# Windowed and latent attention: transposes, rotations and a reciprocal square root take other places in the instruction order

## The reference, cut to what matters

```python
def attn_layer(x, Wqkv, qs, ksc, Wo):
    q, k, v = split(x @ Wqkv)                 # 16 heads of 64
    q = l2norm(q) * qs ; k = l2norm(k) * ksc
    q = q * cos * scale + rotate_half(q) * sin * scale
    k = k * cos / scale + rotate_half(k) * sin / scale
    return local_attention(q, k, v) @ Wo      # softmax over 2 windows of 32
for i in range(6):
    x = attn_layer(shift_tokens(x), ...) + x
    x = ffn_layer(shift_tokens(x), ...) + x   # layer norm, a * gelu(gate)
```

```python
q_c, kv = heads(x) @ W_DQ.T @ W_UQ.T, heads(x) @ W_DKV.T @ W_UKV.T
q = concat(rms_norm(q_c, wq), rms_norm(q_c, wq) @ W_QR.T)
k = concat(rms_norm(k_c, wk), heads(x) @ W_KR.T)
out = softmax(q @ k.T * scale + causal) @ v_c @ W_O.T
```

## Time and profile before

| | |
|---|---|
| median of 3 runs | 6266.62 us (6263.59 to 6266.95) |
| profiled execution | 6259.03 us, span 6257.3 us |
| busy over the span | PE 87%, DVE 68%, ACT 63%, POOL 43% |
| windowed transformer, L1766 first and last start | 642.8 to 5275.1 us |
| latent attention, L1377 first and last start | 5418.5 to 5649.3 us |

### The profile page before, as it was taken

How to read it: one execution, slowest core, us unless ns; L and a number is a source line. 1 busy time by engine, 2 the same in 40 slices (tenths; PEclk the granted TensorE clock), 3 DMA queues, 4 the chain that set the end, 5 groups by cost and what they waited for, 6 DMA issues and landing times. The chain is left out here.

```text
span 6257.3 us, 121573 instructions
## 1 busy us (share of the span) xinstructions
PE 5454.5 (87%) x41154; PEld 3791.3 (61%) x41154; DVE 4256.5 (68%) x16112; ACT 3942.9 (63%) x11510; POOL 2699.1 (43%) x2578
## 2 busy tenths in 40 slices
PE   7885799999999999997489999999999999687989
PEld 5673466666666666665256666666666666454678
DVE  4453777777777877875477777787787777444522
ACT  2211677777777778774177777777777877221333
POOL 0000555555555555552165555555555555220000
PEclk9996899999999999998599999999999999787999
DMA  0000000000000000000000000000000000000000
GB/s 11 22 1 2 21 1 15 6 11 9 7 10 6 11 9 11 8 1 4 21 1 10 9 3 11 9 11 9 1 15 6 11 8 1 5 2 4 2 28 8
DMA packets 30964, 53.45 MB, mean 9 GB/s; under 512 B 7688, under 2 KB 17168, under 8 KB 29712
## 3 DMA queue, kind: packets, MB, share of 16 engines
q1 hardware_dynamic: 30352, 45.66, 2.3%
HBM read 44.60 MB, written 1.05 MB: 7 GB/s over the span
## 5 line engine op out<-in xcount | busy, mean ns | idle before, releaser
L1785 PE MATMUL bank<-wA,next_rowT 128*128 128x512 f32 x2304 | 1185.6, 624 | 272.7 <-DVE turnB L2126 164.0
L1982 ACT ACTIVATE pairs<-pairs,negmax 128x128 f32<-128x128 f32 (+1 forms) x3072 | 1240.4, 420 | 19.0 <-DVE negmax L2087 15.6
L1959 POOL TENSOR_TENSOR turnA<-raw,ropes 128x512 f32<-128x512 f32 x768 | 968.7, 1272 | 243.8 <-ACT raw L2006 214.8
L2087 DVE CUSTOM_DVE_ANT_0 pairs<-bank,bands,big 128x128 f32<-128x128 f32 (+1 forms) x3072 | 941.4, 362 | 86.4 <-PE bank L1717 82.9
L1966 POOL TENSOR_TENSOR qk<-turnA,turnB 128x512 f32<-128x512 f32 x768 | 976.9, 1272 | 0.0
L1785 PEld LDWEIGHTS bank<-wA,next_rowT 128*128 128x128 f32 x2304 | 377.1, 190 | 719.2 <-DVE turnB L2126 378.9
L1943 POOL COPY spread<-recip 128x256 f32<-128x256 f32 x768 | 305.7, 398 | 965.0 <-DVE recip L2096 958.0
L1972 POOL TENSOR_TENSOR qk<-qk,big 128x1024 f32<-128x1024 f32 x192 | 365.6, 1904 | 739.0 <-DVE recip L2201 739.0
L1989 ACT ACTIVATE pairsT<-bank 128x512 f32<-128x512 f32 x768 | 469.2, 611 | 337.3 <-PE bank L1730 337.1
L1982 ACT ACTIVATION_READ_ACCUMULATOR pairs<-pairs,negmax 128x1 f32 x3072 | 631.2, 205 | 0.0
L285 POOL TENSOR_TENSOR rstd<-vareps,neg_half 128x2 f32<-128x2 f32 x56 | 39.0, 696 | 1287.1 <-DVE vareps L256 888.0
(11 more groups left out here) (306 smaller groups left out, 11229.7 us busy)
## 6 DMA issues: line engine op xcount, KB each, us to landing
wA<-in_wt_wqkv SPq DMA_DIRECT2D x72, 256.0 KB, 2.8
wB<-in_wt_wo SPq DMA_DIRECT2D x12, 512.0 KB, 3.5
wC<-in_wt_w SPq DMA_DIRECT2D x12, 341.0 KB, 2.9
wD<-in_wt_w SPq DMA_DIRECT2D x12, 192.0 KB, 2.4
big<-in_e_up SPq DMA_DIRECT2D x1, 2048.0 KB
big<-in_e_down SPq DMA_DIRECT2D x1, 2048.0 KB
scl<-in_wt_scales SPq DMA_DIRECT2D x12, 128.0 KB, 3.1
X<-in_x SPq DMA_DIRECT2D x8, 128.0 KB, 2.5
```

The lines of the kernel that those rows point to most:

```text
L1785: pe.matmul(side_bank(i)[:, :], c.next_rowT[:, t * P:(t + 1) * P], wqkv[:, k * 512:(k + 1) * 512], start=True, stop=True).then_inc(s.chunk ...
L1959: g.tensor_tensor(c.turnA[:, m % 2, :].rearrange("p (h d) -> p h d", h=8), c.raw[:, m % 4, :].rearrange("p (h d) -> p h d", h=8), cos, ALU ...
L1982: last = a.activation(tile, tile, ACT.Exp, scale=-1.0, bias=c.negmax[:, 2 * p + side, t:t + 1], accum_out=c.pair_sums[:, p % 4, t, side:si ...
L2087: last = v.tensor_tensor_reduce(c.pairs[:, 2 * (p % 4) + side, AT[t]:AT[t] + SPAN[t]], c.bank[side][:, AT[t]:AT[t] + SPAN[t]], c.bands[:, ...
```

## The change

Nothing is computed differently, only the order differs. It has four parts.

1. Windowed, VectorE: in slots 1, 2, 4 and 5 the two rotations come ahead of reciprocal, share and turned block.
2. Windowed, VectorE: the first root chain of a turn moves from slot 3 to slot 2.
3. Windowed, PE: `pe_shares` comes ahead of `pe_scores`.
4. Latent: the transposes of q and k (`turn_qk`) move from late in iteration b-2 to the head of iteration b-1, `turn_row` behind the first `flipped`; waits that guard the shared bank are rewired, ScalarE's copies and VectorE's `pick` move with them, and the seventh `take_max` comes ahead of `scale_qk`.

```diff
             def turn_row(b):
-                if ok(b - 2):
-                    pe.wait_ge(core.neg_ready, core.before + b - 1)
-                elif ok(b - 1):
+                if ok(b - 1):
                     pe.wait_ge(core.k_ready, core.before + b)
             def turn_qk(b):
                 pe.wait_ge(normed, b + 1)
-                if ok(b - 3):
-                    pe.wait_ge(added, b - 2)
+                if ok(b - 1):
+                    pe.wait_ge(core.neg_ready, core.before + b)
...
             for b in range(-2, B + 1):
+                if ok(b + 1):
+                    turn_qk(b + 1)
+                flipped(b, 0)
                 if ok(b + 2):
                     turn_row(b + 2)
-                flipped(b, 0)
                 scores(b + 1, 0)
...
                 scores(b + 1, 6)
-                if ok(b + 2):
-                    turn_qk(b + 2)
                 flipped(b, 3)
...
-                take_max(b + 1, 4, 5)
+                take_max(b + 1, 4, 5, 6)
                 if ok(b + 2):
                     scale_qk(b + 2)
-                take_max(b + 1, 6)
+                take_max(b + 1, 7)
                 if ok(b + 3):
                     norm.normalise(v, b + 3)
-                take_max(b + 1, 7)
...
-DVE_RSQRT_SLOTS = {3: 0, 6: 1}
+DVE_RSQRT_SLOTS = {2: 0, 6: 1}
...
                 pe_turn_probs(pe, T, p)
+                if p >= 1:
+                    pe_shares(pe, T, p - 1)
+                elif has_turn(T - 1):
+                    pe_shares(pe, T - 1, PAIRS - 1)
                 if p + 2 < PAIRS:
                     pe_scores(pe, T, p + 2)
...
+                if following:
+                    for m in DVE_ROTATE_SLOTS.get(p, ()):
+                        dve_rotate(v, T + 1, m)
                 dve_recip(v, T, p)
                 if p >= 2:
                     dve_share(v, T, p - 2)
...
                 dve_turn_prev(v, T, p)
-                if following:
-                    for m in DVE_ROTATE_SLOTS.get(p, ()):
-                        dve_rotate(v, T + 1, m)
```

More of the change, by code:

```diff
@@ L1384, in turn_ctx @@
                     pe.wait_ge(squared, 2 * (b + 3) + 2)
+                elif ok(b + 2):
+                    pe.wait_ge(core.k_ready, core.before + b + 3)
                 elif ok(b + 1):
@@ L1393, in maxima @@
             def maxima(b):
-                if ok(b + 1):
-                    pe.wait_ge(core.k_ready, core.before + b + 2)
+                if ok(b - 2):
+                    pe.wait_ge(added, b - 1)
                 else:
-                    pe.wait_ge(added, b - 1)
+                    pe.wait_ge(squared, 2 * (b + 2))
                 core.turn_maxima(pe, core.before + b, side)
@@ L1468, in _ @@
             for b in range(-2, B + 1):
-                if ok(b + 2):
-                    norm.scalar(a, b + 2)
+                if ok(b + 1):
+                    copy_qk(b + 1)
                 for j in range(4):
@@ L1473, in _ @@
                         core.exp(a, core.before + b, j)
+                    if ok(b + 2) and j == 0:
+                        norm.scalar(a, b + 2)
                     if ok(b + 2) and j < HALVES:
                         copy_projection(b + 2, j)
-                    if ok(b + 2) and j == 2:
-                        copy_qk(b + 2)
                 if ok(b + 1):
@@ L1530, in _ @@
             for b in range(-2, B + 1):
+                if ok(b + 1):
+                    v.wait_ge(q_ready, b + 2)
+                    core.pick(v, core.before + b + 1)
                 take_max(b + 1, 0)
@@ L1542, in _ @@
                     norm.statistics(v, b + 3, step)
-                take_max(b + 1, 4, 5)
+                take_max(b + 1, 4, 5, 6)
                 if ok(b + 2):
                     scale_qk(b + 2)
-                take_max(b + 1, 6)
+                take_max(b + 1, 7)
                 if ok(b + 3):
                     norm.normalise(v, b + 3)
-                take_max(b + 1, 7)
-                if ok(b + 2):
-                    v.wait_ge(q_ready, b + 3)
-                    core.pick(v, core.before + b + 2)
 def norm_rows(nc, c):
@@ L1898, in pe_window @@
                 if p >= 1:
-                    pe_shares(pe, T, p - 1)
                     pe_weigh(pe, T, p - 1)
                 elif has_turn(T - 1):
-                    pe_shares(pe, T - 1, PAIRS - 1)
                     pe_weigh(pe, T - 1, PAIRS - 1)
```

## The result

| | before | after |
|---|---|---|
| median of 4 runs | 6265.35 us (6263.59 to 6266.95) | 6420.66 us (6418.17 to 6424.32) |
| profiled execution | 6259.03 us, span 6257.3 | 6422.47 us, span 6420.7 |
| mean clock of the span | 0.95 | 0.921 |

The changed kernel is slower: ratio 1.0248, 95% interval 1.0231 to 1.0266, 155 us by the medians. I had forecast 6417. The account by stages: the two runs of the windowed transformer grew by 97.8 and 92.7 us (each from its first L1766, now L1765, to the addition of its result to the rows, L1596, now L1595), the latent attention lost 26.4, and the rest is 0.7 shorter. That is the 163.4 us between the spans.

The account below looks back on a forecast made before the run. PE was taken to set the windowed turn (busy 43.26 of 46.67 us). 94 turns by (1.0 + 0.8 + 0.1), 179 us, less 29 latent, on 6259.03 gave 6409, with the median's 7.6 us 6417; range 6285 to 6510.

Parts of the forecast that it names:

- The root chain into slot 2: Windowed turn, VectorE: chain meets GpSimd's operations, copy of k and chunk 7 come 3.6 us late, slot 4 3.3 us late.
- The lockout: Slot 2: GpSimd holding VectorE's root chain through their shared ports costs 2.1 us, between ends of 0 and 4.0.
- The rotations first: Windowed slots 4 and 5: all PE waits for rotations are covered, giving back 2.29 us a turn; nothing won in slots 1, 2.
- The turn without its clock: Windowed turn: slot 4 3.3 us late, 2.29 us given back in slots 4 and 5, so 1.0 us longer.
- PE's stall and its clock: Slot 3 stall of 3.6 us lowers PE's clock, costing 0 to 1.46 us a turn; 0.8 taken.
- `pe_shares` ahead: Windowed slots, PE: fills some waits ahead of scores, delays scores elsewhere; -0.2 to +0.4 us a turn, +0.1 taken.
- Latent attention: Latent rows: 3.40 us wait for q and k and 1.46 us of half clock vanish in six rows, 29 us less.
- The clock falls in every turn: Rival, windowed turns: PE's clock drops each turn, 94 by 2.6 less 29, +215 us, 6482; chance 0.12.
- GpSimd does not hold the root chain up: Rival, slot 2: chain and GpSimd miss each other, no stall long enough for the clock, -123 us, 6144; chance 0.13.
- The clock never falls: Rival, windowed turns: PE keeps full clock despite the stall, 94 by 1.1 less 29, +74 us, 6341; chance 0.15.

Follow-up runs that it names:

- the stall filled: Changed kernel with chunk 6 of the projection computed three times instead of once, keeping PE busy ahead of chunk 7: 6281.24 us, ratio 1.0027 to before.
- run 1: Not an experiment: the first of the windowed transformer's two runs within one kernel execution; 97.8 us longer in the changed kernel than in the kernel before.
- the kernel with all four parts in which it doesn't: Changed kernel with GpSimd's cos3 and add2 moved from slot 2 to slot 3: 6100.22 us, ratio 0.9740 to before.
- the two fastest kernels: Changed kernel, copy of k ahead of maxima in slot 3, plus GpSimd's cos3 and add2 in slot 3 (6020.19 us) or rotations first only in slots 4, 5 (6020.96).

## Why the prediction was right, and which of its terms were not

The direction and the path of the harm were right: VectorE's chain, the copy of k, PE's stall, its clock. That the time came within 4 us was luck, since two terms were wrong by about as much in opposite directions.

**The root chain into slot 2: right, step by step.** Counted from the turn's start (1230.43 and 1259.54, 29.11 us apart), the reciprocal comes at 1244.31 where I had put 1244.53, GpSimd's four operations run from 1244.90 to 1250.04 (forecast 1245.1 to 1250.3), L2164 is issued at 1247.06 (1247.4), the chain ends at 1252.19 (1252.4), the next operation after the copy of k starts at 1254.73 (1255.1), and slot 4 starts at 1255.86 (1256.06). One detail was off: L2164 was held for only 0.2 us and two operations of the chain for 1 us each. The lockout is 2.01 us, forecast 2.1. That the chain collides only because the rotations first make GpSimd late was in my working (the row of four operations shifted by 2.5 us), but I called the chain the step that decides. The chain alone gains 67 us.

**The rotations first: right in what goes, wrong in what makes it go.** The waits for rotations in slots 4 and 5 are gone in the changed kernel, as forecast. But the 2.29 us belong to the chain's move: with the chain in slot 2 alone the waits are gone as well, and the rotations alone shorten the turn by 0.41 us.

**The turn without its clock:** forecast +1.0 us. The measured turns average 48.47 (fifteen from 1453.95 to 2180.95), +1.82 over the 46.65 of before; less the clock's 1.52 (48.47 to 46.95, the mean with the stall filled) and without the shares' -0.88, it is +1.18. That is a remainder; no run shows it alone.

**PE's stall and its clock: right kind, size too small.** I took 0.8 us, half of 1.46, because PE was busy before the gap. The clock fell in every turn, 1.52 us on average; in each fifth turn it stayed down longer, through chunk 7 (2.08 us at 1476.90) and to the end of slot 4, and slots 3 and 4 took 1.2 us more than in the others. My upper end of 1.46 was below it. The reason that I gave for a half price doesn't hold.

**`pe_shares` ahead: wrong in size and sign.** I weighed only waits and took +0.1 us a turn, -0.2 at best; it is -0.88. What I named is there and small: a filled wait ahead of the scores (0.21 us in slot 6), and 0.88 instead of 0.67 us ahead of chunk 0. I looked for the cost in who waits for whom, and passed over the 0.17 us between PE's own neighbours, which no wait names: 0.15 us in each of slots 1, 2, 3 and 6.

The sum was right because the errors of the last two terms cancel (0.72 us a turn too small, 0.98 too large): 1.18 + 1.52 - 0.88 = 1.82 us a turn against 1.0 + 0.8 + 0.1 = 1.9. Over 94 turns that is 171 us, and the two runs grew by 190.5: the first turns of each run, where no feed-forward part fills PE, grew by more (run 1: 44.18, 39.13, 40.78 and 45.34 us became 44.12, 46.60, 46.29 and 47.32). I had counted them like the others; they make up 14 of the 19 us.

**Latent attention: right within 3 us,** -26.4 for -29. The wait for q and k is gone. Of the rows shown, one is 28.76 us apart from the next (from 5667.40) and the others 30.3 (one 30.96): in these the wait of 1.21 us for the maxima brings the half clock, in that one it does not (its `flipped` took 0.71 us at 5690.46, against 1.24 at 5719.46). I had not looked for what would be late next.

**The rivals.** "The clock falls in every turn" (chance 0.12) is what the clock did. It was priced at 6482, and the time stayed below it because of the shares: 0.98 us a turn off their forecast, 92 us in all. "GpSimd does not hold the root chain up" was priced at 6144; the kernel with all four parts in which it doesn't measured 6100. "The clock never falls" was priced at 6341, and the kernel with the stall filled measured 6281; the 92 us of the shares are more than the 60 between, and the longer first turns take part of them back.

## What to carry to other kernels

Price a reordering by what each moved wait does to every in-order queue behind it, a second engine's too: here a reciprocal put behind two rotations on VectorE moved GpSimd's work onto a chain of small operations, and four parts worth -205 us together cost +155. Test such a change part by part, and whole with one part left out: the first says what each part is worth, the second which of them collide. One of the two fastest kernels kept all four parts and only moved two of GpSimd's operations and one copy. And look at PE's own neighbours: here each change of tile shape cost 0.17 us that no wait showed.

## What the runs showed of the hardware

- One GpSimd instruction holds one small VectorE operation: 0.17 or 0.18 us became 1.16 to 1.26 us, ending within 0.05 us of it. An operation that arrives between two GpSimd instructions passes (L2143 at 1276.57).
- How often the half clock followed the wait ahead of chunk 7, the first four turns of each run apart: after 3.35 us in every turn, after 2.57 in seven of eight, after some 1.35 in 6 to 9 of 94, after 1.24 (the root chain alone), 1.11 ahead of chunk 8 or 0.19 in none. In the latent part, where PE does other work, it followed a wait of 1.21 us in most rows and in one row not.
- The stall with 1.98 us of needless work in it and 1.63 us left was cheaper by 139 us than the stall of 3.35 us.
- Where the shape of the tile changed from one piece of PE's work to the next, its weight load stood idle for 0.17 us; a slot with one such change fewer was 0.15 us shorter.
